# Decoder layer on one core: weight splits by pairs of FFN tiles, one semaphore per gate tile, context validity on ScalarE, new instruction orders

## The reference, cut to what matters

```python
x = x + attention(layernorm(x), Wqkv, Wo)      # 16 heads of 16, rotary, causal, softmax
x = x + cross(layernorm(x), ctx, ~pad)         # one head of 256; exp of scores; a batch with no valid row gives 0
x = x + ffn(layernorm(x), gate_w, w1, w2, w3, sw1, sw2, sw3)
# ffn: probs = softmax(x @ gate_w.T); comb = probs of the best 2 of 8 experts, 0 elsewhere
#      h = silu(x @ w1[e].T) * (x @ w2[e].T)   # 8 experts of 176 rows and one shared of 352
#      y = sum_e comb[:, e] * (h @ w3[e].T) + shared
```

## Time and profile before

| what | value |
|---|---|
| median of three executions | 286.81 us |
| profiled execution, its own time | 288.7 us |
| its span, first to last instruction | 287.1 us |
| PE busy | 270.9 us (94%) |
| ACT busy | 179.8 us (63%) |
| DVE busy | 159.7 us (56%) |
| POOL busy | 119.7 us (42%) |
| mean granted TensorE clock | 0.986 |

### The profile page before, as it was taken

One profiled execution on the slowest core, in us unless ns is written; L12 is line 12 of the kernel. 1 busy time (PEld: TensorE's weight loads), 2 busy tenths in 40 slices (PEclk: granted clock), 3 DMA queues, 4 the chain that ended last, 5 costly groups with the idle time before them and its releaser, 6 DMA issues.

```text
span 287.1 us, 4943 instructions
## 1 busy us (share of the span) xinstructions
PE 270.9 (94%) x1841; PEld 214.1 (75%) x1841; DVE 159.7 (56%) x349; ACT 179.8 (63%) x304; POOL 119.7 (42%) x133
## 2 busy tenths in 40 slices
...
DMA packets 11879, 17.08 MB, mean 60 GB/s; under 512 B 1904, under 2 KB 8272, under 8 KB 11856
## 3 DMA queue, kind: packets, MB, share of 16 engines
...
HBM read 15.63 MB, written 1.08 MB: 58 GB/s over the span
## 4 chain that ended last, share of the span: by engine, by line
PE 69%; POOL 9%; DMA 6%; ACT 5%; SPq 4%; DVE 3%; issue 2%; DVEq 0%; ACTq 0%; POOLq 0%
PE bank L754 25%; PE bank L767 11%; PE bank L862 11%; PE bank L913 4%; POOL prob_lo L394 3%; DMA gate_raw<-gate 3%; PE bank L808 3%; SPq L270 3%; PE bank L761 3%; PE bank L787 2%; PE bank L794 2%; PE bank L832 2%; DMA comb_b<-comb_dram 2%; POOL w_lo L400 2%; PE bank L812 2%
## 5 line engine op out<-in xcount | busy, mean ns | idle before, releaser
L394 POOL TENSOR_TENSOR prob_lo<-prob,prob_hi 128x1536 f16<-128x1536 f32 x16 | 49.7, 3116 | 18.3 <-ACT prob_hi L516 18.3
L754 PE MATMUL bank<-x_hi,w_hi 128*128 128x512 f32 x112 | 45.9, 410 | 1.0 <-DVE h_c L722 0.9
L551 ACT CAST h_hi<-h_c 128x512 fp32r<-128x512 f32 x28 | 17.4, 620 | 44.0 <-PE bank L862 23.6
L754 PE MATMUL bank<-x_hi,w_lo 128*128 128x512 f32 x112 | 44.2, 395 | 0.0
L754 PE MATMUL bank<-x_lo,w_hi 128*128 128x512 f32 x112 | 44.1, 393 | 0.0
L585 DVE TENSOR_REDUCE negm<-bank 128x2 f32<-128x512 f32 (+1 forms) x48 | 31.5, 686 | 10.0 <-PE bank L789 6.5
L722 DVE TENSOR_TENSOR h_c<-bank,h_s 128x512 f32<-128x512 f32 x28 | 19.3, 689 | 28.4 <-PE bank L754 18.2
L862 PE MATMUL bank<-w_hi,h_hi 128*128 128x256 f32 x112 | 32.5, 290 | 0.3 <-DVE h_lo L736 0.3
L862 PE MATMUL bank<-w_lo,h_hi 128*128 128x256 f32 x112 | 31.7, 283 | 0.0
L862 PE MATMUL bank<-w_hi,h_lo 128*128 128x256 f32 x112 | 31.7, 283 | 0.0
L736 DVE TENSOR_TENSOR h_lo<-h_c,h_hi 128x512 fp32r<-128x512 f32 x28 | 19.7, 705 | 16.7 <-ACT h_hi L551 16.6
(11 more groups left out here) (128 smaller groups left out, 605.0 us busy)
## 6 DMA issues: line engine op xcount, KB each, us to landing
...
```

What stands on the lines that cost most here:

```text
L394: eng.tensor_tensor(prob_lo[:, b % 2], prob[:, b % 2], prob_hi[:, b % 2], ALU.subtract)\
L551: act.copy(h_hi[:, m % 2], h_c[:, m % 2]).then_inc(s["hhi_ok"], 1)
L754: ins = pe.matmul(dst, a(k), c(k), start=(k == 0 and i == 0), stop=(k == kt - 1 and i == 2))
```

## The change

- `up_weights(i)` takes columns 256 * piece to 256 * (piece + 1) of both k halves, two runs of 256, with piece = (i + 5) % 7, so that piece order follows tile order. Counters are separate for w1 and w2. `up.n` of group 0 waits for (n + 1) // 2 + 1 pieces of each, in place of all 14 before `up.0`.
- `comb_b` has one semaphore for each tile j, `cb_in0` to `cb_in10`; the 18 DMAs are issued tile by tile; those of group 1 wait on `hc_ok` tile by tile.
- The validity of a batch is now a scale in ACT's copy of the transposed probabilities (`pt`, Copy becomes Identity with a scale), and `xs_coef` with its DVE instruction is gone.
- The lists are new. No step is added or taken out; PE's fillers go from 29 to 29 `early` and from 20 to 29 `late`.

```diff
 "SP":
-  ... ct.1 cb.0 ct.2 ct.3 cb.1 y.0 y.1
+  ... ct.1 cb.0 ct.2 y.0 ct.3 cb.1 y.1
 "POOL":
-  ... qk.0 ln1.2 sh.0 ln1.3 w12.0 qk.1 w12.1 sh.1 w12.2 qk.2 w12.3 w12.4 qk.3 w12.5 w12.6 sh.2 sh.3 ...
+  ... qk.0 ln1.2 sh.0 qk.1 ln1.3 w12.0 sh.1 qk.2 w12.1 w12.2 w12.3 w12.4 w12.5 w12.6 qk.3 sh.2 sh.3 ...
-  ... ln3.0 qk.7 sh.7 w12.7 h.8 h.9 ln2.1 h.10 w12.8 w12.9 w12.10 w12.11 h.11 w12.12 h.12 ln3.1 h.13 w12.13 h.14 h.15 ...
+  ... ln3.0 h.8 qk.7 sh.7 h.9 w12.7 w12.8 w12.9 ln2.1 h.10 w12.10 h.11 w12.11 w12.12 w12.13 h.12 ln3.1 h.13 h.14 h.15 ...
 "ACT":
-  ... tr.0 tr.1 tr.2 xt.1 tr.3 sh.1 ln1n.2 tr.4 tr.5 sh.2 tr.6 tr.7 sh.3 v.1 mt.0 vm.1 ...
+  ... xt.1 tr.0 tr.1 sh.1 tr.2 tr.3 ln1n.2 tr.4 tr.5 tr.6 sh.2 tr.7 v.1 vm.1 sh.3 mt.0 ...
-  ... pt.0 sh.6 s.24 s.25 tr.24 tr.25 tr.26 ln3n.0 sh.7 tr.27 t3.0 w12.7 tr.28 tr.29 lg.0 tr.30 tr.31 s.26 s.27 h.8 ct.0 s.28 s.29 ot.1 h.9 ...
+  ... pt.0 s.24 s.25 sh.6 s.26 s.27 h.8 tr.24 tr.25 tr.26 tr.27 ln3n.0 sh.7 t3.0 s.28 s.29 tr.28 tr.29 lg.0 tr.30 tr.31 h.9 s.30 ct.0 s.31 w12.7 ot.1 ...
-  ... t3.1 s.45 s.46 h.14 lg.1 s.47 h.15 up.0 ...
+  ... t3.1 s.45 h.14 lg.1 s.46 s.47 h.15 up.0 ...
 "DVE":
-  ... qk.2 m.0 m.1 qk.3 m.2 ... m.11 v.1 vm.1 qk.4 ...
+  ... qk.2 m.0 m.1 m.2 m.3 v.1 qk.3 m.4 ... m.11 vm.1 qk.4 ...
-  ... t3.3 dn.13 lg.3 rk.3 up.14 dn.14 up.15 up.16 y.0 ...
+  ... dn.13 t3.3 y.0 lg.3 rk.3 up.14 dn.14 up.15 dn.15 up.16 ...
 "PE":
-  ... pt.0 pv.7 ro.0 s.24 s.25 qk.7 tr.24 tr.25 s.26 s.27 tr.26 v.3 tr.27 t3.0 tr.28 tr.29 lg.0 tr.30 late.1 tr.31 late.2 m.36 ...
+  ... pt.0 s.24 s.25 ro.0 s.26 s.27 pv.6 qk.7 tr.24 tr.25 pv.7 s.28 tr.26 s.29 tr.27 v.3 t3.0 late.3 pv.8 tr.28 tr.29 lg.0 tr.30 s.30 tr.31 s.31 late.1 m.36 ...
-  ... s.35 m.47 xs.1 mt.3 pv.9 late.4 pv.10 s.36 ...
+  ... m.46 m.47 late.3 mt.3 xs.1 pv.10 s.36 ...
-  ... s.44 s.45 late.2 t3.1 s.46 late.1 pv.12 lg.1 pv.13 s.47 late.2 up.0 ct.1 ...
+  ... s.44 s.45 late.3 t3.1 s.46 late.1 pv.12 lg.1 s.47 pv.13 late.3 up.0 ct.1 ...
-  ... t3.3 dn.11 dn.12 lg.3 up.14 up.15 ct.3 up.16 dn.13 up.17 dn.14 ...
+  ... t3.3 dn.12 dn.13 lg.3 up.14 up.15 ct.3 up.16 dn.14 up.17 dn.15 ...
 def up_weights(i):
-            return [v[:].rearrange("p k n -> p (k n)")[:, i % UPW * 512:(i % UPW + 1) * 512] for v in parts]
+            piece = (i + UPW - 2) % UPW
+            return [v[:, :, 2 * P * piece:2 * P * (piece + 1)] for v in parts]
+        def rows_of(j):
+            cuts = sorted({j * P, (j + 1) * P} | {e * I for e in range(E) if j * P < e * I < (j + 1) * P})
+            return [(r - j * P, q - r, r // I) for r, q in zip(cuts, cuts[1:])]
 def load_comb(g):
-                for e in range(E):
-                    ...
-                            .then_inc(s["cb_in"], 16)
+                for j in range(FE):
+                    if g:
+                        sp.wait_ge(s["hc_ok"], j + FT - FE + 1)
+                    for p0, n, e in rows_of(j):
+                        ...
+                            .then_inc(s[f"cb_in{j}"], 16)
 ACT, pt:
-                    act.copy(tail_t[:], halves_of(ps_tail)).then_inc(s["xph_ok"], 1)
+                    act.wait_ge(s["valid_ok"], 1)
+                    act.activation(tail_t[:], halves_of(ps_tail), ACT.Identity, scale=valid[:, b:b + 1])\
+                        .then_inc(s["xph_ok"], 1)
 DVE, xc and ro:
-                    link(dve.reciprocal(xs_rec[:, :, 0], xs_sum[:]))
-                    dve.wait_ge(s["valid_ok"], 1)
-                    link(dve.tensor_scalar(xs_coef[:, :, 0], xs_rec[:, :, 0], valid[:, b:b + 1], None, ALU.mult))
+                    link(dve.reciprocal(xs_rec[:], xs_sum[:]))
 DVE, up of an expert tile:
-                        dve.wait_ge(s["cb_in"], 16 * CB * (g + 1))
+                        dve.wait_ge(s[f"cb_in{j}"], 16 * len(rows_of(j)) * (g + 1))
 PE, up:
+                    if g == 0 and n < FT - 1:
+                        pe.wait_ge(s["w1_ok"], (n + 1) // 2 + 1)
+                        pe.wait_ge(s["w2_ok"], (n + 1) // 2 + 1)
                     if m == 0:
-                        pe.wait_ge(s["w12_ok"], 2 * UPW)
```

More of the change, by code:

```diff
@@ L74 @@
+        w3.4 w3.5 w3.6 w3.7 w3.8 w3.9 ln2n.2 w3.10 w3.11 w3.12 w3.13 t2.2 up.2 up.3 dn.2 dn.3 xs.2 up.4 pt.2 up.5
+        dn.4 dn.5 ln3n.2 up.6 t3.2 up.7 lg.2 dn.6 dn.7 up.8 ct.2 dn.8 ot.3 up.9 ln2n.3 dn.9 up.10 t2.3 up.11 xs.3
+        up.12 pt.3 dn.10 dn.11 dn.12 up.13 ln3n.3 dn.13 t3.3 lg.3 up.14 up.15 dn.14 ct.3 dn.15 up.16 dn.16 up.17
+        dn.17 up.18 dn.18 up.19 dn.19 up.20 dn.20 up.21 dn.21 up.22 dn.22 up.23 dn.23 up.24 dn.24 up.25 dn.25 up.26
+        up.27 dn.26 dn.27
     """,
     "DVE": """
-        ln1.0 zero.0 zero.1 ln1.1 qk.0 ln1.2 v.0 qk.1 ln1.3 vm.0 qk.2 m.0 m.1 qk.3 m.2 m.3 m.4 m.5 m.6 m.7 m.8 m.9
@@ L77 @@
[L77 to L81, removed]
@@ L82 @@
-        up.6 up.7 lg.2 rk.2 dn.6 dn.7 up.8 dn.8 wo.3 ln2.3 up.9 dn.9 up.10 dn.10 xs.3 xc.3 up.11 up.12 ro.3 ln3.3
-        dn.11 dn.12 up.13 t3.3 dn.13 lg.3 rk.3 up.14 dn.14 up.15 up.16 y.0 dn.15 dn.16 up.17 up.18 dn.17 dn.18 up.19
-        up.20 dn.19 up.21 dn.20 dn.21 up.22 dn.22 up.23 dn.23 up.24 dn.24 up.25 dn.25 up.26 up.27 dn.26 dn.27 y.1
+        ln1.0 zero.0 ln1.1 zero.1 qk.0 ln1.2 v.0 qk.1 vm.0 ln1.3 qk.2 m.0 m.1 m.2 m.3 v.1 qk.3 m.4 m.5 m.6 m.7 m.8
+        m.9 m.10 m.11 vm.1 qk.4 m.12 m.13 m.14 m.15 m.16 m.17 qk.5 m.18 m.19 m.20 pv.0 m.21 m.22 m.23 pv.1 pv.2 pv.3
@@ new lines @@
+        on.0 wo.0 m.24 m.25 ln2.0 m.26 m.27 m.28 pv.4 m.29 m.30 m.31 m.32 v.2 m.33 m.34 m.35 vm.2 xs.0 pv.5 xc.0
+        qk.6 ro.0 ln3.0 pv.6 qk.7 pv.7 on.1 t3.0 pv.8 lg.0 rk.0 m.36 m.37 m.38 m.39 wo.1 ln2.1 m.40 m.41 m.42 m.43
+        m.44 m.45 m.46 m.47 pv.9 v.3 xs.1 vm.3 pv.10 xc.1 pv.11 ro.1 ln3.1 on.2 t3.1 pv.12 lg.1 rk.1 pv.13 up.0
+        pv.14 dn.0 up.1 dn.1 wo.2 ln2.2 pv.15 up.2 up.3 dn.2 xs.2 dn.3 xc.2 up.4 up.5 ro.2 ln3.2 dn.4 dn.5 on.3 t3.2
+        up.6 up.7 lg.2 rk.2 dn.6 dn.7 up.8 dn.8 wo.3 ln2.3 up.9 dn.9 up.10 up.11 xs.3 xc.3 dn.10 up.12 ro.3 ln3.3
@@ L90 @@
[L90 to L99, removed]
@@ L100 @@
-        up.19 up.20 dn.17 up.21 dn.18 dn.19 up.22 dn.20 dn.21 up.23 dn.22 up.24 dn.23 up.25 up.26 up.27 dn.24
-        dn.25 dn.26 dn.27
+        xt.0 qk.0 v.0 qk.1 early.10 xt.1 tr.0 tr.1 qk.2 tr.2 tr.3 v.1 tr.4 tr.5 m.0 m.1 tr.6 m.2 tr.7 m.3 qk.3
+        m.4 m.5 early.7 m.6 m.7 m.8 m.9 m.10 m.11 early.3 mt.0 tr.8 tr.9 xt.2 early.1 tr.10 s.0 s.1 tr.11 tr.12
+        qk.4 tr.13 tr.14 v.2 tr.15 s.2 s.3 m.12 s.4 m.13 m.14 s.5 m.15 s.6 s.7 m.16 m.17 qk.5 m.18 m.19 s.8 s.9
+        pv.0 early.1 m.20 s.10 s.11 m.21 m.22 pv.1 m.23 early.3 mt.1 tr.16 tr.17 pv.2 early.2 tr.18 s.12 s.13
@@ new lines @@
+        tr.19 pv.3 s.14 tr.20 tr.21 s.15 early.2 tr.22 ot.0 tr.23 wo.0 s.16 m.24 m.25 s.17 s.18 m.26 m.27 s.19
+        pv.4 m.28 s.20 s.21 m.29 m.30 t2.0 m.31 s.22 m.32 pv.5 m.33 m.34 s.23 m.35 xs.0 mt.2 xt.3 qk.6 pt.0 s.24
+        s.25 ro.0 s.26 s.27 pv.6 qk.7 tr.24 tr.25 pv.7 s.28 tr.26 s.29 tr.27 v.3 t3.0 late.3 pv.8 tr.28 tr.29
+        lg.0 tr.30 s.30 tr.31 s.31 late.1 m.36 m.37 late.1 ct.0 s.32 ot.1 m.38 m.39 wo.1 m.40 m.41 s.33 pv.9
+        s.34 late.3 m.42 s.35 m.43 m.44 late.1 m.45 t2.1 m.46 m.47 late.3 mt.3 xs.1 pv.10 s.36 s.37 late.2 pt.1
@@ new lines @@
+        s.38 pv.11 ro.1 s.39 s.40 late.1 s.41 s.42 late.1 s.43 late.6 s.44 s.45 late.3 t3.1 s.46 late.1 pv.12
+        lg.1 s.47 pv.13 late.3 up.0 ct.1 pv.14 ot.2 up.1 wo.2 pv.15 up.2 dn.0 dn.1 t2.2 up.3 xs.2 up.4 pt.2 up.5
+        ro.2 dn.2 dn.3 up.6 t3.2 up.7 lg.2 dn.4 dn.5 up.8 ct.2 dn.6 ot.3 dn.7 wo.3 up.9 up.10 t2.3 up.11 xs.3
+        up.12 pt.3 dn.8 dn.9 ro.3 dn.10 up.13 dn.11 t3.3 dn.12 dn.13 lg.3 up.14 up.15 ct.3 up.16 dn.14 up.17
+        dn.15 dn.16 up.18 dn.17 up.19 dn.18 up.20 dn.19 up.21 dn.20 up.22 dn.21 up.23 up.24 dn.22 dn.23 up.25
@@ L224, in decoder_layer @@
         names += ["xn_lo_ok2"]
+        names += [f"cb_in{j}" for j in range(FE)]
         s = {n: sem(n) for n in names}
```

61 lines of the change are left out of this document (24 added, 37 removed).

## The result

The changed kernel takes 285.50 us (median of 20 executions, 284.24 to 288.37) against 286.79 (20 executions, 285.59 to 290.19): a ratio of 0.9949, 95% interval 0.9926 to 0.9972, about 1.5 us less. Forecast: 284.5, in a range of 281.8 to 287.8. Two more comparisons on other chips gave ratios of 0.992 (0.989 to 0.995) and 0.9925 (0.990 to 0.9949): the three ratios put the gain at 1.5 to 2.3 us, their intervals at 0.8 to 3.2. The sign is as forecast, and the forecast of 2.3 us is the top of the three. What the gain is made of is not as forecast.

The account below looks back on a forecast made before the run. PE was taken as the bound, with 69% of the path. The terms -0.6 (start), -0.8 (end of attention) and -0.93 (gate loads) sum to -2.3 us, from 286.81 to 284.5 us, range 281.8 to 287.8.

Parts of the forecast that it names:

- Weight pieces and waits: Before and in the FFN's up tiles: finer waits for weight pieces never bind and extra waits cost nothing, 0.
- double waits: Two extra waits on 13 up tiles in PE's queue: taken as 0, at the far bound 3.0 us lost.
- Validity: Attention: dropping four DVE instructions gains 0; ACT's scaled activation takes about 600 ns, against a 588 ns copy, 0.
- Batch 0's start: Start-up: rot.1 directly after sh.0 brings m.4 to 34.0 in place of 34.62, gain 0.6 us.
- The end of attention: Up to up.0: h.8 made early, h.13 ends 0.25 us earlier, up.0 starts near 143.4; gain 0.8 us.
- h.12's prob_hi moves to about 130.3: ACT's block at the end of attention, at 129.96 before, comes slightly later; POOL takes it at 131.8, not 132.00.
- Gate loads: FFN group 1: tile 0 needs only its first DMA, so PE's hole of 0.93 us goes; group 0 gives 0.
- The signs: Checks by time: up.0 at 143 to 143.8, h.13's end at 138.5 to 140; wrong if up.0 after 144.2 or before 142.
- The Faster rival: Nine more fillers keep the clock up before up.0 and more of the start's lead stays: 282.0 us, chance 0.15.
- No gain: Batch 3's delay cancels start and attention gains, extra waits take back the gate gain: 286.6 us, chance 0.18.

Follow-up runs that it names:

- e4: The changed code with the step lists of the kernel before; 285.98 us, ratio 0.9936.
- e2: The kernel before with only the gate part: one semaphore per gate tile, loads issued tile by tile; 285.56 us, ratio 0.9929.
- e3: The code of the kernel before with the new step lists; 299.52 us, ratio 1.0407.
- e9: The changed kernel again without an edit, on another chip; 284.76 us, ratio 0.9925.
- e7: The changed kernel with POOL's gate-weight split and mask conversion (tr.7) moved from before the first rotary sum to behind sh.3; 283.99 us, ratio 0.9896.
- e5: The changed kernel with xs_rec at its old size and an unused xs_coef, so later buffers lie where they lay before; 284.37 us, ratio 0.9906.
- e8: The changed kernel with nine late fillers taken out between t3.0 and m.45 on PE; 284.77 us, ratio 0.9935.
- e10: The changed kernel with both the edits of e5 and e7; 283.73 us, ratio 0.9900.
- e6: The changed kernel with t2.1 ahead of h.11 on ACT and xs.1 earlier on PE and DVE; 287.69 us, ratio 1.0031.
- e11: e10 with 4 in place of 10 matmuls on zeros before the second batch-0 transposes; 285.59 us, ratio 0.994.

## Why the prediction was right, and which steps were not

- **Weight pieces and waits, 0: right.** tr.8 to up.0 is 103.10 before and 103.13 in e4. The bound of 3.0 us for double waits came nowhere near: from up.0 to the end e4 is 0.42 us longer than e2, the longer step included.
- **Validity, 0: right in the sum, wrong in the size of the activation.** 684 ns in place of about 600, 0.10 more than the copy, four times; in e4 none of it reaches up.0. The Trainium skill (SBUF — State Buffer, "Who interferes with whom") would have the DVE instruction blocked only until POOL's instruction, which holds the shared ports, ends. The trace agrees: batch 1's took 2,465 ns in e2, beside a prob_lo block, and 270 ns in e3, where the lists put it elsewhere; both ended within 0.03 us of the POOL instruction that was running, and with POOL idle it took 228.
- **Batch 0's start, -0.6: right, and low.** -0.77 in the two profiled executions, both at the low clock there; -1.25 at full clock (e2 20.86, e9 19.58 to e7 19.61). m.4 was forecast at 34.0 and came at 34.43, in an execution that began 0.56 late. In front of rot.0 both kernels wait for a late DMA (the mask's); I had read past it, and e7 took that wait away.
- **The end of attention, -0.8: this step failed.** From tr.8 to up.0 after loses 0.30 us, and e5, e7, e8 and e10 lie within 0.1 of the kernel before, though they had the full clock ahead of up.0 and it had not. So the new lists gain nothing there, and may lose up to about 0.5 us. The fault is in "h.12's prob_hi moves to about 130.3". It came at 130.78, 89.9 us behind tr.8, while 130.3 is 89.2 behind the old one. What I put too low is what xs.1 behind mt.3 on PE does to ACT, which waits 1.16 us for its maxima; one other order, e6, was worse. The list of signs was also at odds with the sum: the times that give the 0.8 had no lead of the start in them, so with both gains up.0 was due at 142.8, not at the 143 to 143.8 of the list.
- **Gate loads, -0.93: right, and low.** -1.16 in e2. In group 0, where I put 0, the new lists would lose 4.08 us without the semaphores (e3).
- **A term that was missing: +0.57,** the step of the up tiles (e5).
- **The signs.** "I am wrong if up.0 starts later than 144.2 or before 142" came true in both ways: 144.28 in the trace of after and 141.74 in e9, the same kernel. h.13 ended at 140.21, outside 138.5 to 140. Such bounds, counted from the first instruction, can't judge a change of 2 us where the first transposes of one kernel begin at 18.46 or 19.98 us.
- **The Faster rival** had its mechanism half right. A mean clock of 0.997 or more came in 19 of 74 executions of the kernel before and in 23 of 40 of the changed one, and such executions are shorter than those at 0.99 to 0.997 by 0.6 to 1.7 us (medians). But it isn't the nine added late fillers that do it (e8). The Trainium skill (TensorE: Matmul & The Clock Gate, "What's actually happening") has activity lift the clock. At the start the trace agrees (0.73 us of idle and 1.00 in e10, 1.81 and 0.75 in e11); near up.0 no run here shows what decides.

**No gain** was right for the end of attention only.

By pieces: -1.2 (start, at full clock), 0 (end of attention, as the traces stand), -1.16 (gates), +0.57 (step) is -1.8 us, against ratios that say -1.5 to -2.3. That the forecast of -2.3 came near is luck: two terms were too small, where one was too large and one was missing.
